# Routed expert outputs added to the tokens' rows in DRAM tile by tile, and a quantised layer's queries projected as whole numbers

## What is computed

```python
def _qdq(x):
    s = jnp.maximum(jnp.max(jnp.abs(x), axis=-1, keepdims=True) / 127.0, 1e-08)
    return jnp.clip(jnp.round(x / s), -127.0, 127.0) * s
q = _qdq(x) @ _qdq(wq).T + bq            # layer 2, x is the normalised residual
```

```python
for each token: x += gate * sum over its 2 experts of weight * expert(layernorm(x))
# layer 2: expert width 256;  layer 3: expert width 352, and a dense shared expert of width 1408 beside them
```

## Time and profile before

| | |
|---|---|
| median of 3 runs | 3220.0 us |
| profiled execution | 3227.43 us, span 3225.7 us |
| mean granted TensorE clock | 0.921 of 2.4 GHz |
| PE busy | 2710.5 us (84%) |
| DVE / ACT / POOL busy | 1733.3 / 1175.1 / 918.3 us |
| DMA | 232.26 MB, mean 72 GB/s |

### The profile page before, as it was taken

How to read it: one execution, slowest core, us unless ns; L and a number is a source line. 1 busy time by engine, 2 the same in 40 slices (tenths; PEclk the granted TensorE clock), 3 DMA queues, 4 the chain that set the end, 5 groups by cost and what they waited for, 6 DMA issues and landing times. The chain is left out here.

```text
span 3225.7 us, 35731 instructions
## 1 busy us (share of the span) xinstructions
PE 2710.5 (84%) x11415; PEld 1641.4 (51%) x11415; DVE 1733.3 (54%) x3048; ACT 1175.1 (36%) x2510; POOL 918.3 (28%) x436
## 2 busy tenths in 40 slices
PE   7998797999764599999699988588589988699895
PEld 3555585644232365565454543266454543477563
DVE  2454675477657899893655653411555653444212
ACT  0111221466625788780144444111134443222110
POOL 0000000488331010100056663112257663221112
PEclk9989898999986799999799998789799997899998
DMA  6220222332200100100332120332532220212623
GB/s 222 80 96 23 72 75 83 92 78 60 53 30 0 53 27 27 52 27 13 103 70 66 34 60 17 139 142 86 148 70 51 49 60 17 79 40 101 207 65 112
DMA packets 101257, 232.26 MB, mean 72 GB/s; under 512 B 22512, under 2 KB 27120, under 8 KB 99696
## 3 DMA queue, kind: packets, MB, share of 16 engines
q1 hardware_dynamic: 88624, 189.46, 19.6%
q0 software_dynamic: 12480, 40.90, 3.8%
HBM read 142.74 MB, written 30.67 MB: 54 GB/s over the span
## 5 line engine op out<-in xcount | busy, mean ns | idle before, releaser
L1567 POOL TENSOR_TENSOR L_attn_total<-L_attn_total,L_attn_probs 128x2048 f32<-128x2048 f32 x120 | 546.3, 4552 | 163.2 <-ACT L_attn_probs L1522 158.9
L1601 DVE TENSOR_REDUCE L_attn_row_max<-L_attn_rows_ps 128x1 f32<-128x512 f32 x512 | 336.9, 684 | 274.6 <-PE L_attn_rows_ps L1407 271.5
L1522 ACT ACTIVATE L_attn_probs<-L_attn_s_ps 128x512 f32<-128x512 f32 x512 | 292.8, 596 | 427.5 <-PE L_attn_s_ps L1427 424.2
L1427 PE MATMUL L_attn_s_ps<-L_attn_q_stack,L_attn_k_stack 98*128 98x512 f32 (+1 forms) x768 | 382.4, 534 | 39.3 <-DMA L_attn_q_stack<-L_attn_ml 33.5
L477 PE MATMUL L_ffn_hidden<-L_ffn_x_high,L_ffn_up_high 128*128 128x512 f32 x688 | 295.2, 429 | 102.6 <-DVE L_ffn_routes L393 54.4
L359 ACT ACTIVATE L_ffn_sums<-sims 128x128 f32<-128x128 f32 x1024 | 315.5, 389 | 47.3 <-DVE L_ffn_routes L379 26.9
L1567 POOL TENSOR_TENSOR L_attn_total<-L_attn_probs 128x2048 f32<-128x2048 f32 x20 | 91.0, 4551 | 796.5 <-ACT L_attn_probs L1522 796.5
L1427 PEld LDWEIGHTS L_attn_s_ps<-L_attn_q_stack,L_attn_k_stack 98*128 98x128 f32 (+1 forms) x768 | 144.1, 197 | 267.7 <-issue 132.4
L477 PE MATMUL L_ffn_hidden<-L_ffn_x_low,L_ffn_up_high 128*128 128x512 f32 x688 | 272.6, 396 | 0.0
L1407 PE MATMUL L_attn_rows_ps<-L_attn_k_stack,L_attn_q_stack 96*128 96x512 f32 x512 | 212.9, 451 | 28.3 <-DVE L_attn_row_max L1601 25.6
L1440 PE MATMUL L_attn_o_ps<-L_attn_probs,L_attn_values 128*32 128x512 f32 x1536 | 212.9, 627 | 27.1 <-ACT L_attn_probs L1522 22.9
(11 more groups left out here) (276 smaller groups left out, 4321.9 us busy)
## 6 DMA issues: line engine op xcount, KB each, us to landing
L_attn_k_stack<-L_attn_kh SPq DMA_DIRECT2D x192, 128.0 KB, 2.3
L_attn_ctxT<-in_ctxT SPq DMA_DIRECT2D x8, 2048.0 KB, 10.8
L_attn_abs_in<-in_L_ffn_w SPq DMA_DIRECT2D x12, 1024.0 KB, 9.1
L_attn_k_stack<-L_attn_kl SPq DMA_DIRECT2D x96, 128.0 KB, 2.3
L_attn_q_stack<-L_attn_qh SPq DMA_DIRECT2D x192, 64.0 KB, 2.0
L_ffn_xg<-x_slots POOLq DMA_DIRECT2D x46, 256.0 KB, 3.2
y_slots<-L_ffn_y_sb POOLq DMA_DIRECT2D x46, 256.0 KB, 2.3
L_ffn_up_all<-in_L_ffn_w SPq DMA_DIRECT2D x16, 704.0 KB, 12.2
```

What stands on the lines that cost most here:

```text
L1427: nc.tensor.matmul(s_ps[:, v % S_SLOTS, :], k_stack[0:depth, n % 2, h, kt * P:(kt + 1) * P], q_stack[0:depth, n % 2, h, :], start=True, st ...
L1522: nc.scalar.activation(probs[:, g % P_SLOTS, h, :], s_ps[:, v % S_SLOTS, :], ACT.Exp, **kinds).then_inc(exp_done, 1)
L1567: nc.gpsimd.tensor_tensor(total[:], first, probs[:, g % P_SLOTS], ALU.add).then_inc(added, 1)
L1601: nc.vector.tensor_reduce(row_max[:, r // HALVES_K, r % HALVES_K:r % HALVES_K + 1], rows_ps[:, r % R_SLOTS, :], AX_X, ALU.max, negate=True ...
```

## The change

1. **Sums in DRAM.** `routed_block` no longer keeps `y_slots`. At its start SP stores `env.x` to `sums` (2 MB; in layer 3 `sums` is the output itself). For each slot tile DVE multiplies the result by the tile's weights while it copies it, and POOL adds its rows to the tokens' rows in DRAM with one indirect DMA that accumulates (`add_y`). Each such DMA waits until the one before has landed. Rows of padding carry the token number 1024 and fall to the bounds check. Layer 2 at the end loads the 8 tiles back into `env.x`; layer 3 is done.
2. **Rows carry their token.** A row of `x_slots` has 517 values in place of 512: token number, and for each pick expert and weight. DVE makes each tile's token column and weights from them (`weigh`, 4 small instructions). Each layer has its own `x_slots`, so SP writes 46 blank tiles in place of 23 in layer 0.
3. **Queries from whole numbers.** In layer 2 the tokens and the query weights keep their whole numbers, are held as fp32r, and the product is multiplied afterwards by both steps: one more DVE instruction per set (`q_scaled`) before ACT's `high`, which then reads SBUF. The tokens' steps are spread over the partitions at the end of `norm_block` (8 diagonal matrices on DVE, 8 products with ones on PE, 2 copies on ACT).

```diff
@@ norm_block
-                        quantise_rows(nc, link, xn[:, t % 4:t % 4 + 2, :], xn[:, t % 4:t % 4 + 2, :], top, tmp)
+                        quantise_rows(nc, link, xn[:, t % 4:t % 4 + 2, :], xn[:, t % 4:t % 4 + 2, :], top[:, :, t:t + 2], tmp,
+                                      whole=(0, 1))
                         dve.sem_inc(xn_done, 2)
+                        for u in (t, t + 1):
+                            nc.vector.tensor_scalar(diagonal[:, u, :], env.ident[:], top[:, 0, u:u + 1], None,
+                                                    ALU.mult).then_inc(diagonal_done, 1)
@@ PE
+                    for t in range(TILES):
+                        pe.wait_ge(diagonal_done, t + 1)
+                        last = nc.tensor.matmul(steps_ps[:, t * P:(t + 1) * P], ones[:], diagonal[:, t, :], start=True, stop=True)
+                        if t % 4 == 3:
+                            last.then_inc(spread_done, 1)
@@ ACT
+                    for h in range(HALVES):
+                        act.wait_ge(spread_done, h + 1)
+                        nc.scalar.copy(env.x_steps[:, h * HALF:(h + 1) * HALF], steps_ps[:, h * HALF:(h + 1) * HALF]).then_inc(
+                            steps_copied, 1)
+                    act.wait_ge(steps_copied, HALVES)
@@ class Slots
-        self.rows = sb("rows", [P, TILES, D])
+        self.rows = sb("rows", [P, TILES, ROW])
@@ routed_block, SP
+                sp.dma_start(sums.rearrange("(t p) d -> p t d", p=P), env.x[:]).then_inc(kept, 16)
                 load_weights(sp)
+                sp.wait_ge(kept, 16)
+                sp.wait_ge(summed, 16 * I)
+                if not last:
                     for t in range(TILES):
+                        sp.dma_start(env.x[:, t, :], sums[t * P:(t + 1) * P, :]).then_inc(back[t], 16)
@@ POOL
                 def load_x(i):
                     if i >= XS:
                         pool.wait_ge(x_turned, i - XS + 1)
+                        pool.wait_ge(weighed, i - XS + 1)
+                    nc.gpsimd.dma_start(xg[:, i % XS, :], slots.x_slots[i * P:(i + 1) * P, :]).then_inc(x_loaded[i % XS], 16)
+                def add_y(i):
                     pool.wait_ge(y_copied, i + 1)
-                    nc.gpsimd.dma_start(env.y_slots[i * P:(i + 1) * P, :], y_sb[:, i % YS, :]).then_inc(stored[i % YS], 16)
+                    if i:
+                        pool.wait_ge(summed, 16 * i)
+                    else:
+                        pool.wait_ge(kept, 16)
+                    nc.gpsimd.indirect_dma_start(
+                        sums, bass.IndirectOffsetOnAxis(ap=token[:, i:i + 1], axis=0), y_sb[:, i % YS, :], None,
+                        bounds_check=TOK - 1, oob_is_err=False, compute_op=ALU.add).then_inc(summed, 16)
-                for t in range(TILES):
-                    for p in range(PICKS):
-                        nc.gpsimd.indirect_dma_start(
-                            taken[p][:, t, :], None, env.y_slots,
-                            bass.IndirectOffsetOnAxis(ap=slots.place[:, p, t:t + 1], axis=0)).then_inc(back[PICKS * t + p], 16)
@@ DVE
                     if i >= YS:
-                        dve.wait_ge(stored[i % YS], 16 * (i // YS))
-                    nc.vector.tensor_copy(y_sb[:, i % YS, :], y_ps[:]).then_inc(y_copied, 1)
+                        dve.wait_ge(summed, 16 * (i - YS + 1))
+                    nc.vector.tensor_scalar(y_sb[:, i % YS, :], y_ps[:], tile_weight[:, i:i + 1], None, ALU.mult).then_inc(
+                        y_copied, 1)
@@ streamed_attention_block, DVE low(n, i)
+                    if whole and not key:
+                        b, f = n % BATCH, n // BATCH
+                        product = ql[:].bitcast(F32)
+                        dve.wait_ge(product_done, place[n, i] + 1)
+                        nc.vector.scalar_tensor_tensor(product, bank(n, i), env.q_step[:, f:f + 1],
+                                                       env.x_steps[:, b * SEQ:(b + 1) * SEQ], ALU.mult, ALU.mult).then_inc(
+                                                           q_scaled, 1)
+                        dve.wait_ge(q_scaled, n + 1)
@@ linear_attention_block, SP
-                for i in range(SLOT_TILES):
-                    sp.dma_start(env.x_slots[i * P:(i + 1) * P, :], blank[:]).then_inc(blank_stored, 16)
+                for x_slots in env.x_slots.values():
+                    for i in range(SLOT_TILES):
+                        sp.dma_start(x_slots[i * P:(i + 1) * P, :], blank[:]).then_inc(blank_stored, 16)
```

More of the change, by code:

```diff
@@ L863, in _, with routed_block @@
                 dve.sem_inc(slots.placed, 1)
-def routed_block(env, name, slots, weights, load_weights, E, out=None):
+def routed_block(env, name, slots, weights, load_weights, E, sums, last):
     nc = env.nc
@@ L1040, in _ @@
                 copy_y(I - 1)
-                for t in range(TILES):
-                    for p in range(PICKS):
-                        n = PICKS * t + p
-                        dve.wait_ge(back[n], 16)
-                        if p:
-                            dve.wait_ge(added, n)
-                        nc.vector.scalar_tensor_tensor(env.x[:, t, :], taken[p][:, t, :], slots.weight[:, p, t:t + 1],
-                                                       env.x[:, t, :], ALU.mult, ALU.add).then_inc(added, 1)
-                    if out is None:
-                        dve.wait_ge(added, PICKS * (t + 1))
+                if not last:
+                    for t in range(TILES):
+                        dve.wait_ge(back[t], 16)
                         env.tile_stats.take(env, dve, t)
-                dve.wait_ge(added, PICKS * TILES)
-                if out is None:
                     env.tile_stats.finish(dve)
@@ L2280, in expert_layer @@
                     down_sb = down_tile()
-                    routed_block(env, name, slots, (up_sb, down_sb), all_down, E, last)
+                    routed_block(env, name, slots, (up_sb, down_sb), all_down, E, sums, last)
                 else:
@@ L2291, in expert_layer @@
                             nc.psum_tensor(f"{name}_logits_ps", [P, HALVES, HALF], F32) as slots.logits_ps:
-                        norm_block(env, name, rows=slots.rows, router=slots,
+                        norm_block(env, name, rows=slots.rows[:, :, 0:D], router=slots,
                                    early_loads=lambda sp: slots.load_router(env, sp))
@@ L2296, in expert_layer @@
                                               "gpsimd": lambda pool: slots.scatter(env, pool)}, slots)
-                    routed_block(env, name, slots, (up_sb, down_sb), lambda sp: None, E)
+                    routed_block(env, name, slots, (up_sb, down_sb), lambda sp: None, E, sums, last)
         if "L0_attn" in stages:
@@ L2342, in build @@
         if "L3_ffn" in stages:
-            expert_layer("L3_ffn", env.tanh_gates[:, 7:8], io["L3_ffn_shared_w1"].shape[0], False, out.rearrange("b (t p) d -> p (b t) d", p=P))
+            expert_layer("L3_ffn", env.tanh_gates[:, 7:8], io["L3_ffn_shared_w1"].shape[0], False,
+                         out.rearrange("b s d -> (b s) d"), last=True)
         else:
```

140 lines of the change are left out of this document (93 added, 47 removed).

## The result

The changed kernel takes 3228.35 us (median of 14 runs, 3219.24 to 3232.44), the kernel before 3221.85 us beside it (14 runs, 3215.51 to 3231.76). The ratio is 1.0023, 95% interval 1.0012 to 1.0033: within the 0.5% that I counted as no change, on the slow side of it, and 52 us away from the forecast of 3176. All ratios here are of fast runs, and one execution of p_sums, of 11512.74 us, is left out of them.

A forecast was written before the change was run, and what follows sets the result against it. PE was taken to pace the routed blocks and layer 2's attention, with PE-free tails of gathers and adds. Terms -26.0 - 13.5 + 2.5 + 1.0 - 13.0 + 5.0 = -44.0 us, from 3220 to 3176 us, range 3164 to 3190.

The forecast's parts named there:

- the queries: Layer 2's attention: shorter query projections save 2.0 us per set in six sets; -13 us in all, from 0 to -18.
- the scaling ends near 1707.7, before ACT asks, and costs nothing: Layer 2's attention: DVE's added 0.75 us instruction fits its idle time; 0 us, up to 0.7 per set at risk.
- the chain costs nothing in either loop: Routed loops of layers 2 and 3: an add every 4.8 us stays below the 5.83 and 8.08 us tile pace; 0 us.
- S: Routed blocks: time from issue start of one accumulating indirect DMA to its landing; taken as 4.5 us, between 2.8 and 5.75.
- layer 3's start: Start of layer 3's routed block and its router chain: +1 us.
- The tail of layer 2: End of layer 2: last add lands, SP loads 2 MB back, statistics done at 2266.8 against 2280.25; -13.5 us, ends 11 and 17.
- The tail of layer 3: End of kernel: gathers and adds go, span ends after the last add lands, near 3199.7; -26.0 us.
- Layer 2's start: Start of layer 2's routed block, DMA engines full: 2 MB store queues beside first slot loads; +2.5 us, from 0 to 8.
- The normalisation: Layer 2's normalisation: added diagonals on DVE, products on PE and an ACT copy paid in full; +5 us, +3 to +7.
- B: Rival: the add chain paces layer 2, 5 us in the loop, 2.5 per tail; 3186, up to 3203 us; chance 0.16.
- D: Rival: the queries give nothing, PE's freed time becomes waits for DVE, normalisation is paid; 3189 us; chance 0.14.
- C: Rival: an add's rows do not overlap, 8.5 us each; 3262 us; chance 0.06 above 8.1 us, 0.05 for 7 to 8.1.

The follow-up runs named there:

- p_sums: Kernel before plus only the sums in DRAM (router block, routed block, layer 0's blanks), queries as before; 3209.68 us, ratio 0.9959 to the kernel before.
- e1_psum: Changed kernel with the scaled query written back into its PSUM bank instead of the SBUF tile of the low part; 3201.68 us, ratio 0.9943 to before.
- e8_old_q: p_sums with the edits of e3_four and e6_defer, so the queries of the kernel before; 3181.89 us, ratio 0.9885 to before.
- e7_three: Changed kernel with the edits of e1_psum, e3_four and e6_defer together; 3175.26 us, ratio 0.9852 to before.
- e2_sp_loads: Changed kernel with layer 2's slot tiles loaded by SP from its own queue instead of by POOL; 3207.67 us, ratio 0.9953 to before.
- e3_four: Changed kernel with four slot tile buffers instead of three in both layers; 3203.36 us, ratio 0.9935 to before.
- e4_noacc: Changed kernel with accumulation taken out of the indirect DMAs, which overwrite the tokens' rows, so sums are left out; one run, 3201.27 us.
- e6_defer: Changed kernel with layer 3's down weights of experts 3 to 7 issued one by one as slot tiles are turned; 3220.80 us, ratio 1.0002 to before.

## Why the prediction was wrong

**Where it failed, 1: the queries (-13.0 forecast; +15 with the normalisation's share taken off).** The step is "the scaling ends near 1707.7, before ACT asks, and costs nothing". The scaling did cost nothing: in e1_psum it is there as well, and the sets are shorter than before. But I priced the instruction that was added and not the one whose operands moved: the diff has the subtraction read `ql`, a tile of SBUF, in place of the bank, and I kept its 0.75 us. It takes 4.43 beside POOL's adds; the earlier trace rows has POOL busy 33.19 of 50 us, so the odds of meeting one were in my own rows. It delays the join of the row maxima and with it the fold, for which PE waits 3.8 us longer per set and then runs at half clock for some us (0.50 from 1720 to 1724, back to 0.93 from 1724 to 1732). e1_psum settles it. Beside this the saving itself was mis-sized: I kept 2.0 us per set for the shorter projections, and with the stall gone it is 0.9 to 1.1 (e8_old_q against e7_three, and the earlier trace rows against e1_psum). The granted clock over the five sets was 0.96 in e7_three and 0.99 in e8_old_q, which by itself would be some 1.4 us per set, an estimate; no run separates it from DVE's share.

**2: inside the loop of layer 2 (0 forecast, +19.0).** The step is "the chain costs nothing in either loop", and behind it "`load_x` of tile i+3 is queued on POOL behind the add of i-1, two tiles ahead of its use". I named the load and gave it a cover of two tiles without working it out. The load waits in the program for the tile that frees its buffer, so its lead is 4.2 us, not two steps. S was nearly right (4.7 against 4.5), and the chain of adds did have cover, though less than the 1.0 us I gave it, for I took 0.3 us until POOL starts the next one and it is 0.8; it was the load behind each add that had no cover for what the add does to it. e2_sp_loads and e3_four settle it from two sides, e4_noacc names the accumulation as what makes the add and the load behind it late.

**3: layer 3's start (+1.0 forecast, +6.3).** I charged the 2 MB store to layer 2's start and nearly nothing to layer 3's, where the same store meets 5.5 MB of down weights. e6_defer shows that the backlog is the cause.

**Right in mechanism, off in size.** The tail of layer 2: -15.7 for -13.5, and this is in part luck: the last adds write no rows and land in 2.75 us. With full tiles at 4.7 it would be near -12, an estimate. I had not asked what the last tiles hold. The tail of layer 3: -23.0 for -26.0; the last add is issued 1.8 us after the start of the last copy as forecast (1.9), but the span ends 7.8 us after that issue and not 4.8. That add writes no rows either, and such a one landed in 2.75 in layer 2; what the other 5 us are, the profile does not show, and it stays open. It is not the accumulation: in e4_noacc the span ends 7.3 us after the last issue. In the kernel before it ended 3.4 us after DVE's last add (3222.29). Layer 2's start: +1.3 for +2.5. The normalisation: +1.2 for +5.0. Its products end 3.6 us later than before (I had worked out 5 with ACT's copy), and the first projection then needs less time. Timeline of the changed kernel, which answers to the earlier trace rows:

```profile
1562.05 3.18 PE L227 MATMUL L_attn_steps_ps<-L_attn_norm_diagonal,L_attn_norm_ones 128*128 128x128 f32 x16
1566.51 7.10 PE L1440 MATMUL L_attn_product_ps<-L_attn_ctxT,L_attn_wk 128*128 128x512 f32 x16 [1.28 <-PEq L150]
```

7.10 us for 9.56: between 1562 and 1570 the granted clock is 0.84 where it was 0.64. The prediction had the 7.0 and the reason, and did not put it into the sum.

**Right.** Layer 0's blanks are free: the 46 stores keep SP until 75.1, and the next group's weights are issued at 102.2 as before. DVE's `weigh` instructions lie in its idle time.

**The rivals.** None of them was it. The three failed terms are 28, 19 and 5 us off, together 52; the other terms of the table are together 4 us better than forecast. B had the right stage and the wrong wait: it let the adds pace the loop, at 5 us plus 5; what paced it was the load in the same queue, at 19. By the Trainium skill ("DMA: Bandwidth & Descriptors", Anatomy of one DMA — SWDGE (gpsimd) path), whose fit of 2.0 us plus the bytes over 436 GB/s I had counted twice, an add would take some 6.5 us, an estimate; a full one takes 4.7, so the trace puts it well below. D gave the queries a worth of nothing, at 3189, and did not go below nothing. C's add of 8 us is far off. I had no rival in which two parts lose at once, and the chance of "same" was 0.08.

## What to carry to other kernels

When a diff gives an instruction a new source, price that instruction again with its new operands, and look at what the other engines do at that time; an instruction that is not in the diff's added lines can be the one that gets nearly six times as long. When a slower transfer goes onto a queue, the price is not its own chain alone but that of every load behind it: work out each one's lead from the wait that releases it, not from its number of buffers. And a bulk store put at the start of a stage that already fills the DMA engines is paid by the first small transfers behind it. Before you read a price off the last instruction of a loop, look at how many bytes it moved: here the cleanest-looking adds were the empty ones.

## What the runs showed of the hardware

- A DVE instruction of 0.75 us with both inputs in SBUF took 4.43 us while POOL added two SBUF tiles (4.5 us each); with one of the inputs in PSUM it took 0.75 beside the same adds.
- An accumulating indirect DMA of up to 128 rows of 2 KB: issue 1.6 us, landing 4.7 (median), with a load behind it in the queue or without one (e2_sp_loads). Without the accumulation: 1.0 and 2.8. One whose rows all fell to the bounds check still took 2.75 us to land.
- A load of 258.5 KB on POOL's queue lands in 4.9 us behind an accumulating DMA, in 3.2 behind a plain scatter; on SP's queue beside the accumulating ones it lands in 2.6. Rows of 2068 bytes were no slower than rows of 2048 in the loop.
- POOL started these indirect writes 0.8 us after the copy that they wait for had ended, with and without accumulation, a plain store 0.3 us.
